# Differential attention: value products one more head behind the scores, a ring of eight half heads

## The chip, the cores and the metric

The kernel runs on one core of a Trainium2 chip, as one launch. The metric is the device time in microseconds of that launch, the median of several runs.

## The reference

The program is two layers of a hybrid network over 8 sequences (B) of 512 tokens (T) with 256 channels (C): differential attention, routed local attention with experts, a state-space layer, experts again, a fully connected layer with quantised weights and a last attention. The change touches the first part alone, which computes, for 8 heads of two half heads each (16 channels per half head) with H = 8 and hd = 16:

```
q, k = apply_rotary(rmsnorm(x @ Wq.T)), apply_rotary(rmsnorm(x @ Wk.T))   # per half head
v = (x @ Wv.T).reshape(B, T, H, 2 * hd)
scores = where(causal, q @ k.T / sqrt(hd), -inf)
attn = softmax(scores)                       # (B, 2H, T, T)
attn = attn[:, :, 0] - lam * attn[:, :, 1]   # two half heads of one head
out = layernorm(attn @ v) * (1 - LAMBDA_INIT)
x = x + out.reshape(B, T, C) @ Wproj.T       # x is a layer norm of the residual on the way in
```

The softmax has no maximum in the kernel: it takes exponentials of the scores, and a column of ones beside v gives the sums.

## The kernel before

`diff_attention` is one block in which each engine runs its own program in order, with semaphores between them. All loops go over **slots**: slot s stands for half head s, 16 slots for a batch element (called a batch below), 128 for all. A job of batch b stands at slot 16 b plus an offset from a table; the offsets reach from -39 to 32, so three batches are in work at a time. In the text a cycle slot is a slot modulo 16.

TensorE (PE), per slot s, in this order:

- scores of head s // 2 + 1, in three units of two half heads each (L270): units 0 and 1 in even slots, unit 2 in odd ones. Two pairs of PSUM banks alternate, so a unit waits for the exponentials of the unit two before it.
- in even slots, between the units, the value products of one head (L285, 16 matmuls): before the change those of head (s - 2) // 2. They wait for the triangle masks of both half heads and for the copy of the head before it out of the one PSUM bank that they use.
- the odd jobs of the slot. They use three "odd" PSUM banks in turn, in the order of the sorted job list, so each job waits until the bank of the job three places ahead of it is emptied. The jobs: x (transpose the normalised rows, L299), qk and v (products of three float32r terms, L138), turn (transpose q and k, L316), back (transpose a head's value sums to tokens, L321), heads (transpose the attention result, L326), out (product with Wproj, L332).

ScalarE (ACT), per slot: first it empties the odd banks filled in the slot before (x L378, qk L385, v L390, the high part of a turn L397, heads L400), then it copies the value sums of a head (`heads_out`, L365), then come the roots (logarithm and exponential for rms, row and head norms, L406 to L421), then the exponentials of the slot's score units into the ring `pt` (L358). A ring entry is waited for until the value products that read it are done. The high part of turn n waits for the spill DMAs of turn n - 2, since `hi` and `lo` have two buffers.

GpSimd (POOL), per slot: its jobs (cast of x L584, squares of q and k into one buffer L590, rotary swaps L599, the stack DMAs L610 that bring spilled q and k back), and then the masks of one half head, `triangle(s + 1)`, L576 and L578.

VectorE (DVE), per slot: it empties the odd banks of the slot before (low part of a turn L453, back L460 to L468, out into the residual L472 and, after the second, the row statistics), then its jobs: statistics and normalisation of rows (L112), low part of x (L491), sums of squares (L498), the scaling of q and k (L506), rope (L511, L515), and the norm of the heads: mean (L522, L524), centre (L528), square (L532), var (L536) and scale (L540, L542).

SyncE issues the six spill DMAs of each turn (L248), and clears regions of memory for a later stage.

Around the change, the end of a batch's preparation is a run over three engines: in cycle slot 11 ScalarE computes the rms root (L411, L416); VectorE scales q and k in slots 12 and 13; GpSimd swaps in slots 13, 13, 14 and 15, and issues stack DMAs in slot 15 ahead of the fourth swap; VectorE does rope in slots 14 and 15 and normalises the next batch's rows in 15; in slot 16 it adds the first output product to the residual. The sorted odd jobs from cycle slot 13 on are, before the change: heads 0, heads 1, back (13); out 0, back (15); out 1, v 0 (16); back, v 1 (17); turn 0, x 0, x 1 (18); back, turn 1 (19); turn 2 (20); back, turn 3, qk 0 (21). After it: heads 0, heads 1, back (13); out 0, back (15); out 1 (16); back (17); v 0, turn 0, x 0, x 1 (18); back, v 1, turn 1 (19); turn 2 (20); back, turn 3, qk 0 (21).

Of the kernel before, what the change touches and what calls it, by code (L numbers as in the profile page):

```python
# [27 lines left out]
B, T, C = 8, 512, 256  # L28
# [98 lines left out]
DA_H = 8  # L127
# [15 lines left out]
def diff_attention(core, w, a, spill, beside, s_x, load_rows, load_tables):  # L143
# [5 lines left out]
    nc, ps = core.nc, core.ps  # L149
    NH = 2 * DA_H  # L150
    NS = B * NH
    RING, CHUNKS = 6, 4
    S_BANK, AV_BANK, ODD_BANK, NODD = 0, 4, 5, 3
    place_of = (0, 640, 1024, 512)
    unit_tiles = ((0,), (3, 1), (2,))
    units = ((0, T), (T, 2 * T), (2 * T, 2 * T + 2 * P))
    table = [(-30, "x", 0), (-30, "x", 1), (-27, "qk", 0), (-26, "qk", 1), (-25, "qk", 2), (-24, "qk", 3),
             (-16, "v", 0), (-15, "v", 1), (-14, "turn", 0), (-13, "turn", 1), (-12, "turn", 2), (-11, "turn", 3),
             (29, "heads", 0), (29, "heads", 1), (31, "out", 0), (32, "out", 1)]
    table += [(2 * hv + 5, "back", hv) for hv in range(DA_H)]  # L160
    vector_table = [(-39, "stats", 0), (-33, "normal", 0), (-28, "xlo", 0), (-25, "sum", 0), (-24, "sum", 1), (-23, "sum", 2), (-22, "sum", 3),
                    (-20, "rms", 0), (-20, "scaled", 0), (-20, "scaled", 1), (-19, "scaled", 2), (-19, "scaled", 3),
                    (-18, "rope", 0), (-18, "rope", 1), (-17, "rope", 2), (-17, "rope", 3),
                    (20, "mean", 0), (21, "centre", 0), (22, "square", 0), (23, "var", 0), (27, "scale", 0)]
    scalar_table = [(-37, "row", 0), (-21, "rms", 0), (27, "std", 0)]
    pool_table = [(-29, "xhi", 0), (-26, "square", 0), (-25, "square", 1), (-24, "square", 2), (-23, "square", 3),
                  (-19, "swap", 0), (-19, "swap", 1), (-18, "swap", 2), (-17, "swap", 3),
# [18 lines left out]
    with own, ctx:  # L186
        def sb(name, shape, dt=F32):
            return ctx.enter_context(nc.sbuf_tensor("da_" + name, shape, dt))
# [21 lines left out]
        mean, var = sb("mean", [P, NT * DA_H]), sb("var", [P, NT * DA_H])  # L210
# [19 lines left out]
        def filled(eng, job):  # L230
            eng.wait_ge(s_odd, place[job] + 1)

        with nc.Block() as block:
# [22 lines left out]
            def _(pe):  # L256
                def scores(hv, u):
                    b, h = divmod(2 * hv, NH)
                    g, p = h // 8, h // 2 % 4
                    if h % 8 == 0 and u == 0:  # L260
                        for i in (2 * g, 2 * g + 1):
                            pe.wait_ge(s_stack[i], 32 * (b + 1))
                    unit = 3 * hv + u
                    if unit >= 2:
                        pe.wait_ge(s_e, 2 * (unit - 1))
                    for j in unit_tiles[u]:
                        c0 = place_of[j] % T
                        for sub in range(2):
                            r = 64 * sub
                            last = nc.tensor.matmul(ps[:, S_BANK + 2 * (unit % 2) + sub, c0:c0 + T - j * P],  # L270
                                                    kT[g][r:r + DA_ROWS, p, j * P:(j + 1) * P],
                                                    qT[g][r:r + DA_ROWS, p, j * P:T], start=True, stop=True)
                    last.then_inc(s_s, 1)

                def values(hv):
                    b, h = divmod(hv, DA_H)
                    pe.wait_ge(s_tri, 2 * (2 * hv + 2))
                    if h == 0:
                        pe.wait_ge(s_v, 2 * b + 2)
                    if hv >= 1:  # L280
                        pe.wait_ge(s_osb, hv)
                    for j in range(NT):
                        for sub in range(2):
                            c0 = place_of[j]
                            last = nc.tensor.matmul(ps[64 * sub:64 * sub + 64, AV_BANK, j * P:T],  # L285
                                                    vx[b % 2][:, j, h, :], pt[:, (2 * hv + sub) % RING, c0:c0 + T - j * P],
                                                    start=(j == 0), stop=(j == NT - 1))
                    last.then_inc(s_av, 1)
# [48 lines left out]
                for s in range(first_slot, last_slot):  # L337
                    ahead = 0 <= s + 2 - s % 2 < NS
                    if ahead:
                        scores(s // 2 + 1, 2 * (s % 2))  # L340
                    if s >= 2 and s % 2 == 0 and (s - 2) // 2 < B * DA_H:
                        values((s - 2) // 2)
                    if ahead and s % 2 == 0:
                        scores(s // 2 + 1, 1)
                    for job in odd.get(s, ()):
                        fill(job)

            @block.scalar
            def _(act):
# [11 lines left out]
                def heads_out(hv):  # L361
                    act.wait_ge(s_av, hv + 1)
                    if hv >= 2:
                        filled(act, ("back", (hv - 2) // DA_H, (hv - 2) % DA_H))
                    nc.scalar.copy(osb[:, hv % 2, :], ps[:, AV_BANK, :]).then_inc(s_osb, 1)  # L365
# [37 lines left out]
                def root(kind, b):  # L403
                    if kind == "row":
                        act.wait_ge(s_mv, b + 1)
                        nc.scalar.activation(core.std[:, b, :], core.mv[:, b, :, 1], ACT.Ln, bias=core.eps[:, :], scale=1.0)  # L406
                        act.drain()
                        nc.scalar.activation(core.rstd[:, b, :], core.std[:, b, :], ACT.Exp, scale=-0.5).then_inc(s_std, 1)
                    elif kind == "rms":
                        act.wait_ge(s_sum, NT * (b + 1))  # L410
                        nc.scalar.activation(ssum[:, :, :], ssum[:, :, :], ACT.Ln, bias=core.rms_eps[:, :],  # L411
                                             scale=1.0 / DA_D)
                        act.drain()
                        if b:
                            act.wait_ge(s_qn, NT * b)
                        nc.scalar.activation(srcp[:, :, :], ssum[:, :, :], ACT.Exp, scale=-0.5).then_inc(s_rms, 1)  # L416
                    else:
                        act.wait_ge(s_var, b + 1)
                        nc.scalar.activation(var[:, :], var[:, :], ACT.Ln, bias=core.eps[:, :], scale=1.0 / 32)
                        act.drain()  # L420
                        nc.scalar.activation(var[:, :], var[:, :], ACT.Exp, scale=-0.5).then_inc(s_std2, 1)  # L421
# [8 lines left out]
                for s in range(first_slot, last_slot):  # L430
                    for job in odd.get(s - 1, ()):
                        empty(job)
                    if s >= 3 and (s - 3) % 2 == 0 and (s - 3) // 2 < B * DA_H:
                        heads_out((s - 3) // 2)
                    for kind, b, i in scalar_jobs.get(s, ()):
                        if kind != "row" or b:
                            root(kind, b)
                    if 0 <= s + 2 - s % 2 < NS:
                        for u in ((0, 1), (2,))[s % 2]:
                            exponentials(s // 2 + 1, u)  # L440
# [3019 lines left out]
```

## Time and profile before

| | us |
|---|---|
| median of 3 runs (4077.23 to 4085.93) | 4081.86 |
| the profiled execution | 4082.73 |
| its span | 4080.9 |
| TensorE matmul busy in the span | 3623.4 (89%) |
| VectorE busy | 2915.8 (71%) |
| ScalarE busy | 1929.7 (47%) |
| GpSimd busy | 1633.9 (40%) |
| mean granted TensorE clock, of full speed | 0.949 |

Busy shares are over all stages. The first stage is the first seventh of the span. Matmuls are pipelined, so busy TensorE time overlaps itself.

### The profile page before, as it was taken

To read this page: it belongs to the slowest core of one execution; us is meant where nothing else is said; L and a number is where in the kernel's file an instruction comes from. 1 tells how busy PE (TensorE), PEld (TensorE's weight loads), DVE (VectorE), ACT (ScalarE), POOL (GpSimd) and SP (SyncE) were. 2 spreads that over 40 slices of the span, in tenths; PEclk is the share of its full clock that TensorE was granted. 3 is DMA by queue.
4 is the path that set the end of the run, shared out by engine and by line. 5 is a ranking of instruction groups with operands and counts; after the bars stand their busy time and mean duration, and the time that the engine had idled before them with its cause. 6 is when DMAs were issued, how large, how long until landed. Compare 5 with 4: busy or idle time off the path is not lost. (4 is left out here: it accounts for less than half of the span.)

```text
span 4080.9 us, 60197 instructions
## 1 busy us (share of the span) xinstructions
PE 3623.4 (89%) x19256; PEld 2605.9 (64%) x19256; DVE 2915.8 (71%) x5355; ACT 1929.7 (47%) x4079; POOL 1633.9 (40%) x1485
## 2 busy tenths in 40 slices
PE   4888878999599999998799788987999899999998
PEld 3455557889488888887789634544666455554666
DVE  5777657676566666645677578886888676766998
ACT  3565644444455555544344344442444466656332
POOL 3776726454566666633555411101003445441000
PEclk8999979999899999998899889989999899999999
DMA  5999902565100000001266400002102444441000
GB/s 136 303 256 275 304 32 73 167 202 170 48 19 17 19 19 19 19 2 38 95 186 195 154 24 17 19 11 43 21 0 49 91 111 101 103 110 25 11 15 16
DMA packets 228874, 358.33 MB, mean 88 GB/s; under 512 B 36482, under 2 KB 132851, under 8 KB 221811
## 3 DMA queue, kind: packets, MB, share of 16 engines
q1 hardware_dynamic: 204038, 265.38, 22.4%
q0 software_dynamic: 24544, 89.36, 9.0%
q8 instruction: 147, 2.41, 0.3%
q14 instruction: 145, 1.18, 0.1%
HBM read 173.82 MB, written 172.20 MB: 85 GB/s over the span
## 5 line engine op out<-in xcount | busy, mean ns | idle before, releaser
L2895 DVE TENSOR_REDUCE ab_nmx<-banks 128x1 f32<-128x512 f32 x512 | 329.3, 684 | 136.6 <-PE banks L2682 134.2
L2826 ACT ACTIVATE ab_pt<-banks 128x512 f32<-128x512 f32 x512 | 283.2, 600 | 162.0 <-PE banks L2692 152.9
L1737 POOL TENSOR_TENSOR lb_pq<-lb_pq,lb_rr 128x512 f32<-128x512 f32 x192 | 206.2, 1077 | 305.1 <-DVE lb_rr L1598 301.7
L1463 ACT ACTIVATE lb_pq<-banks,lb_nmx 128x256 f32<-128x256 f32 x384 | 178.5, 470 | 230.0 <-DVE lb_nmx L1593 226.8
L2692 PE MATMUL banks<-ab_qT,ab_kT 128*128 128x512 f32 x512 | 253.2, 500 | 5.3 <-ACT ab_pt L2826 5.3
L358 ACT ACTIVATE da_pt<-banks 128x512 f32<-128x512 f32 (+1 forms) x384 | 179.1, 537 | 123.4 <-PE banks L270 119.1
L1593 DVE TENSOR_REDUCE lb_nmx<-banks 128x2 f32<-128x512 f32 x192 | 131.1, 683 | 146.5 <-PE banks L1315 145.2
L2682 PE MATMUL banks<-ab_kT,ab_qT 128*128 128x512 f32 x512 | 209.1, 411 | 18.5 <-DVE ab_nmx L2895 13.7
L285 PE MATMUL banks<-da_pt,da_vx 128*64 128x512 f32 (+3 forms) x1024 | 166.3, 470 | 34.4 <-POOL da_pt L578 30.8
L576 POOL TENSOR_TENSOR da_pt<-da_pt,w_da_tri 128x384 f32<-128x384 f32 x128 | 150.4, 1175 | 87.0 <-ACT da_pt L358 86.9
L2466 PE MATMUL banks<-w_f_dT,f_hT 128*128 128x256 f32 x768 | 178.3, 382 | 4.0 <-ACT f_hT L2512 4.0
L2692 PEld LDWEIGHTS banks<-ab_qT,ab_kT 128*128 128x128 f32 x512 | 98.0, 193 | 131.1 <-ACT ab_pt L2826 77.2
L928 ACT ACTIVATE moe_b_h_raw<-banks,moe_b_b 128x512 f32<-128x512 f32 x124 | 85.0, 688 | 196.2 <-PE banks L138 165.5
L928 ACT ACTIVATE moe_a_h_raw<-banks,moe_a_b 128x512 f32<-128x512 f32 x124 | 84.7, 688 | 196.5 <-PE banks L138 163.3
L2441 PE MATMUL banks<-w_f_gT,f_xT 128*128 128x512 f32 (+1 forms) x512 | 169.6, 474 | 6.1 <-DVE f_both L2555 3.1
L2466 PEld LDWEIGHTS banks<-w_f_dT,f_hT 128*128 128x128 f32 x768 | 146.8, 192 | 38.1 <-ACT f_hT L2512 5.2
L2441 PE MATMUL banks<-w_f_uT,f_xT 128*128 128x320 f32 (+1 forms) x512 | 161.9, 459 | 0.0
L285 PEld LDWEIGHTS banks<-da_pt,da_vx 128*64 128x64 f32 x1024 | 76.5, 145 | 126.5 <-issue 77.5
L2490 ACT ACTIVATE f_sg<-banks 128x704 f32<-128x704 f32 x64 | 48.5, 758 | 205.2 <-PE banks L2441 205.2
L138 PE MATMUL banks<-moe_a_w_hi,moe_a_h_hi 128*128 128x256 f32 x496 | 144.0, 290 | 0.0
L138 PE MATMUL banks<-moe_b_w_hi,moe_b_h_hi 128*128 128x256 f32 x496 | 144.0, 290 | 0.0
L138 PE MATMUL banks<-moe_b_w_lo,moe_b_h_hi 128*128 128x256 f32 x496 | 141.3, 285 | 0.0
(538 smaller groups left out, 11180.4 us busy)
## 6 DMA issues: line engine op xcount, KB each, us to landing
moe_xs<-zero SPq DMA_DIRECT2D x71, 512.0 KB, 11.5
moe_ys<-zero SPq DMA_DIRECT2D x71, 512.0 KB, 11.5
moe_a_w_raw<-in_moe_w SPq DMA_DIRECT2D x48, 512.0 KB, 3.9
moe_b_w_raw<-in_moe_w SPq DMA_DIRECT2D x48, 512.0 KB, 3.8
da_spill<-da_hi SPq DMA_DIRECT2D x128, 128.0 KB, 2.4
ab_spill<-ab_hi SPq DMA_DIRECT2D x128, 128.0 KB, 2.4
ab_qT<-ab_spill POOLq DMA_DIRECT2D x32, 392.0 KB, 5.8
ab_kT<-ab_spill POOLq DMA_DIRECT2D x32, 392.0 KB, 5.5
```

Of the source, the lines that this page charges most:

```text
L138: done = core.nc.tensor.matmul(bank, a[i], b[j], start=(first and n == 0), stop=(last and n == len(terms) - 1))
L285: last = nc.tensor.matmul(ps[64 * sub:64 * sub + 64, AV_BANK, j * P:T], vx[b % 2][:, j, h, :], pt[:, (2 * hv + sub) % RING, c0:c0 + T - j ...
L358: nc.scalar.activation(pt[:, n % RING, c0:c1], ps[:, S_BANK + 2 * (unit % 2) + sub, 0:c1 - c0], ACT.Exp, scale=1.0 / math.sqrt(DA_D)).then ...
L928: nc.scalar.activation(h_raw[:, m % 2, :], ps[:, UP_BANK + n % 3, :], ACT.Gelu, bias=b1[:, load_of[i] % 2, m:m + 1]).then_inc(s_g, 1)
L1463: nc.scalar.activation(pq[:, n % RING, t, :], ps[:, S_BANK + n % 2, 2 * P * t:2 * P * t + 2 * P], ACT.Exp, bias=nmx[:, n % RING, t:t + 1], ...
L1737: nc.gpsimd.tensor_tensor(pq[:, n % RING, :, :], pq[:, n % RING, :, :], bcast(rr[:, n % RING, :], 2, 2 * P), ALU.mult).then_inc(s_p, 1)
L2441: last = nc.tensor.matmul(ps[:, bank, at:at + size], self.xT[:, k, c, :], w[key][:, c, c0:c0 + size], start=(c == 0), stop=(c == KC - 1))
L2466: last = nc.tensor.matmul(ps[:, 3, 0:C], self.hT[:, k, m, :], w["f4_dT"][:, m, :], start=False, stop=(m == F4_IC - 1))
L2682: nc.tensor.matmul(ps[:, MAX_BANK + n % 3, :], half.q[:, par, p, qt * P:(qt + 1) * P], half.k[:, p, :], start=True, stop=True).then_inc(s_ ...
L2692: nc.tensor.matmul(ps[:, EXP_BANK + n % 3, :], half.k[:, p, j * P:(j + 1) * P], half.q[:, par, p, :], start=True, stop=True).then_inc(s_s, 1)
L2826: nc.scalar.activation(pt[:, s % RING, :], ps[:, EXP_BANK + s % 3, :], ACT.Exp, scale=AB_D ** -0.5).then_inc(s_e, 1)
L2895: nc.vector.tensor_reduce(nmx[:, g % 2, col:col + 1], ps[:, MAX_BANK + n % 3, :], op=ALU.max, axis=AX.X, negate=True).then_inc(s_mx, 1)
```

## The change

The ring of exponentials has eight entries instead of six. The value products of a head, its copy by ScalarE and its transposes back come two slots (one head) later relative to the scores. The two v products of a batch, and mean, centre, square and var of the head norm, also stand two slots later; scale and the jobs behind it stay.

```diff
-    RING, CHUNKS = 6, 4
+    RING, CHUNKS = 8, 4
...
-             (-16, "v", 0), (-15, "v", 1), (-14, "turn", 0), (-13, "turn", 1), (-12, "turn", 2), (-11, "turn", 3),
+             (-14, "v", 0), (-13, "v", 1), (-14, "turn", 0), (-13, "turn", 1), (-12, "turn", 2), (-11, "turn", 3),
...
-    table += [(2 * hv + 5, "back", hv) for hv in range(DA_H)]
+    table += [(2 * hv + 7, "back", hv) for hv in range(DA_H)]
...
-                    (20, "mean", 0), (21, "centre", 0), (22, "square", 0), (23, "var", 0), (27, "scale", 0)]
+                    (22, "mean", 0), (23, "centre", 0), (24, "square", 0), (25, "var", 0), (27, "scale", 0)]
...
-                    if s >= 2 and s % 2 == 0 and (s - 2) // 2 < B * DA_H:
-                        values((s - 2) // 2)
+                    if s >= 4 and s % 2 == 0 and (s - 4) // 2 < B * DA_H:
+                        values((s - 4) // 2)
...
-                    if s >= 3 and (s - 3) % 2 == 0 and (s - 3) // 2 < B * DA_H:
-                        heads_out((s - 3) // 2)
+                    if s >= 5 and (s - 5) % 2 == 0 and (s - 5) // 2 < B * DA_H:
+                        heads_out((s - 5) // 2)
```

## Rows read from the trace of the kernel before

**Rows 1.** The page: span and number of instructions.
```profile
span 4080.9 us, 60197 instructions
```
**Rows 2.** Waits of TensorE, 85 to 500 us: total us, times, longest.
```profile
PE banks L285 <- POOL da_pt L578: 30.6, 14, 4.9
PE banks L138 <- DVE residual L472: 7.9, 5, 2.5
PE banks L138 <- DVEq L455: 6.8, 6, 2.4
```
**Rows 3.** Timeline of TensorE, 303 to 331: start, duration, idle before.
```profile
304.54 2.37 PE L285 MATMUL banks<-da_pt,da_vx 128*64 128x512 f32 x16 [0.30 <-POOL da_pt L578]
...
314.31 3.69 PE L285 MATMUL banks<-da_pt,da_vx 128*64 128x512 f32 x16 [4.01 <-POOL da_pt L578]
...
322.95 0.39 PE L138 MATMUL banks<-da_wv_hi,da_xT_hi 128*128 128x256 f32 x1 [2.54 <-DVE residual L472]
323.18 0.28 PE L138 MATMUL banks<-da_wv_lo,da_xT_hi 128*128 128x256 f32 x1
323.30 0.28 PE L138 MATMUL banks<-da_wv_hi,da_xT_lo 128*128 128x256 f32 x1
```
**Rows 4.** Timeline of GpSimd, 299 to 324.
```profile
304.44 3.41 POOL L599 TENSOR_TENSOR da_rot<-da_qk,w_da_sin 128x512 f32<-128x512 f32 x2
...
310.41 1.59 POOL L599 TENSOR_TENSOR da_rot<-da_qk,w_da_sin 128x512 f32<-128x512 f32 x1 [0.68 <-issue]
...
314.20 1.05 POOL L610 DMA_DIRECT2D da_qT<-da_spill  x2
...
316.27 1.28 POOL L599 TENSOR_TENSOR da_rot<-da_qk,w_da_sin 128x512 f32<-128x512 f32 x1
```
**Rows 5.** Timeline of VectorE, 299 to 324.
```profile
317.58 1.89 DVE L511 TENSOR_TENSOR da_qk<-da_qk,w_da_cos 128x512 f32<-128x512 f32 x1 [2.78 <-POOL da_rot L599]
...
322.22 0.68 DVE L472 TENSOR_TENSOR residual<-banks,residual 128x512 f32<-128x512 f32 x1
```
**Rows 6.** TensorE in a stretch: bounds, length, busy, granted clock, DMA share, GB/s.
```profile
193.00:197.00 4.00, 4.00 (x16) 0.50 1.05 408
```
**Rows 7.** Timeline of TensorE, 126 to 152.
```profile
133.02 3.89 PE L285 MATMUL banks<-da_pt,da_vx 128*64 128x512 f32 x16 [4.18 <-POOL da_pt L578]
...
141.78 0.39 PE L138 MATMUL banks<-da_wv_hi,da_xT_hi 128*128 128x256 f32 x1 [1.88 <-DVE da_t L463]
...
148.16 0.66 PE L316 MATMUL banks<-ident,da_qk 128*128 128x128 f32 x4
```
**Rows 8.** Timeline of TensorE, 430 to 446.
```profile
438.65 4.54 PE L285 MATMUL banks<-da_pt,da_vx 128*64 128x512 f32 x16 [4.92 <-POOL da_pt L578]
```
**Rows 9.** VectorE by line, 85 to 500: count, busy us, mean ns, idle before.
```profile
L528 DVE TENSOR_TENSOR da_att<-da_att,da_mean 128x1024 f32<-128x1024 f32 x6 | 9.9, 1647 | 0.8
```
**Rows 10.** Timeline of VectorE, 282 to 300.
```profile
291.77 1.09 DVE L498 TENSOR_REDUCE da_ssum<-da_sq 128x32 f32<-128x512 f32 x1 [1.27 <-POOL da_sq L590]
...
296.93 1.07 DVE L498 TENSOR_REDUCE da_ssum<-da_sq 128x32 f32<-128x512 f32 x1
```
**Rows 11.** Timeline of ScalarE, 294 to 302.
```profile
299.16 0.39 ACT L411 ACTIVATE da_ssum<-da_ssum,rms_eps 128x128 f32<-128x128 f32 x1
```
**Rows 12.** Timeline of TensorE, 456 to 468.
```profile
462.22 2.37 PE L285 MATMUL banks<-da_pt,da_vx 128*64 128x512 f32 x16 [1.62 <-ACT da_osb L365]
```
**Rows 13.** Timeline of TensorE, 71 to 95.
```profile
85.59 3.71 PE L285 MATMUL banks<-da_pt,da_vx 128*64 128x512 f32 x16 [3.00 <-POOL da_pt L578]
...
90.20 1.04 PE L299 MATMUL banks<-ident,x_normed 128*128 128x128 f32 x8
```
**Rows 14.** Timeline of VectorE, 85 to 92.
```profile
86.01 3.28 DVE L112 TENSOR_SCALAR x_normed<-residual,mean_var,rstd 128x256 f32<-128x256 f32 x4
```
**Rows 15.** Timeline of VectorE, 527 to 546.
```profile
536.08 0.20 DVE L460 RECIPROCAL da_rr<-banks 128x8 f32<-128x8 f32 x1
...
537.36 1.22 DVE L522 TENSOR_REDUCE da_mean<-da_att 128x32 f32<-128x1024 f32 x1
```

## The prediction, made before the changed kernel ran

> **What bounds the kernel now.** I read the page's span first, then the waits of TensorE inside the first stage, then the timelines of TensorE, GpSimd, VectorE and ScalarE over one batch. The change touches only the first stage, differential attention, in a span of 4080.9 us [rows 1]. TensorE works nearly without a break there, and its largest idle group is the value products waiting for the triangle masks of GpSimd: 30.6 us in 14 waits; behind it stand 7.9 us for VectorE's residual add and 6.8 us for a bank that VectorE empties [rows 2]. So the change aims at the largest wait. The question is whether that wait is the cause or only the first place at which TensorE meets something late.
>
> In one batch [rows 3]: the value products of cycle slot 14 start at 304.54, those of slot 16 at 314.31 after 4.01 us of idling, and TensorE idles again, 2.54 us, before the v product at 322.95. GpSimd in the meantime is not idle. It works through the rotary swaps with the masks queued between them: two swaps from 304.44 for 3.41 us, a third at 310.41, then the issue of four stack DMAs from 314.20 to 316.27, and the fourth swap, done at 317.55 [rows 4]. VectorE waits 2.78 us for that swap, runs rope and the normalisation of the next rows, and only then, at 322.22, adds the output product to the residual, which frees an odd bank at 322.90 [rows 5]. I call this run, from the roots on ScalarE in slot 11 to the residual add in slot 16, the ladder. Both waits of TensorE are waits for the same ladder, the first part way along, the second at its end.
>
> **The change part by part.**
>
> *Value products two slots later, ring of eight.* Value products of slot 16 now need the masks made two pool slots earlier (before the swaps that start at 304.44), so the 4.0 us wait goes, in each of the six ladders. The count of products, exponentials and masks stays. The two added ring entries keep the wait of the exponentials for a free entry at the same slot distance.
>
> What is late next: the odd banks rotate by three in the order of the job list. Before, the v product (slot 0) stood three behind output product 0, and so waited for the residual add. After, that place belongs to the transposes back of slot 1. TensorE was ready for the slot 16 values at 314.31 - 4.01 = 310.30. They take 2.37 us at the full clock (as at 304.54). Scores and output product behind them took from 318.00 (314.31 + 3.69) to 320.41 (322.95 - 2.54), so 2.4 us; the score unit of slot 17 is 0.4. TensorE arrives at the bank at 315.5 and waits until 322.9, some 7.4 us [rows 3]. GpSimd and VectorE have the same instructions in the same order within the ladder, and none of them waits for TensorE there (VectorE's one wait is for GpSimd), so nothing ends it earlier. The gain per batch is only what TensorE does before the new wait and did behind the old one: one score unit, 0.4 us.
>
> *The clock.* After each of the six 4 us waits TensorE ran at its half level: a window of 4 us after one of them has a granted clock of 0.50 (1.2 of 2.4 GHz) [rows 6]. The value products there took 3.89 us in the first and 4.54 us in the last of six [rows 7, 8], 4.2 in the mean, instead of 2.37 [rows 3]: 1.8 us lost. So far this is hidden, because TensorE idles for the ladder's end 2.5 us afterwards. With one wait of 7 us at the end of the ladder the slow products come behind it, and from there to the next roots TensorE sets the pace. Cost +1.8 per batch, less 0.3 for the slow v products that one batch already had. Bounds: 0 to +2.7 (all of the next 6 us slow).
>
> The Trainium skill, "TensorE: Matmul & The Clock Gate", section "Why this matters for your kernels", warns of idle gaps of TensorE between bursts of matmuls, after which it runs at its lower clock. The rule speaks against a change that joins two gaps into one long one with work right behind it: by it the five regular ladders cost their 1.8 us each, while with a clock that does not mind the gap the sum below would be 9 us lower. The trace agrees with the rule (0.50 after the 4.0 us gap).
>
> *Statistics two slots later.* mean, centre, square, var move from cycle slots 4 to 7 to slots 6 to 9, among the four sums of squares and the row statistics. They add mean (1.22 [rows 15]) and centre (1.65 [rows 9]) plus a small multiply and drains, 3.2 us, ahead of the fourth sum. VectorE idled 1.27 us there for GpSimd's square, and the fourth sum ended at 298.00, 1.16 us before the root that reads it [rows 10, 11]. 3.2 - 1.27 - 1.16 = 0.8 us by which roots, and with them the ladder, start later. The square buffer is single, so GpSimd's squares shift too, but the masks queued behind them now have two slots to spare. Five ladders have this: +4.0 (bounds 0 and 3.6 each, if shared-port slowing stretches all four). ScalarE's wait for var has two slots left, enough in the loop.
>
> *v products two slots later.* v0 joins the turn and x jobs in slot 2, v1 those in slot 3; ScalarE's two copies move along. The x cast on GpSimd now waits for v1 of slot 3, about when the x copies end plus one product; the low part on VectorE is needed two slots later, so I cost this at nothing. If that cover is gone it is at most 1.5 us per batch. v1 now lies between turn 0 and turn 2, whose high part waits for the spill DMAs of turn 0. TensorE's waits for turn 2's bank, 6.8 us in six and up to 2.4 [rows 2], fall to a floor of some 0.65 (exponentials and subtraction): -2.9. In the last batch with turns, the value products waited 1.62 us behind ScalarE, which had waited for the same DMA [rows 12]: -1.3.
>
> *The first ladder* has no output products yet. There TensorE waited at 141.78 for a bank and started turn 0 at 148.16 [rows 7]; after the change turn 0 is what waits, and starts near 141.8, with v1 still to come (twelve matmuls 0.12 us apart, 1.4 us [rows 3]) and 1.8 slow: -3.2.
>
> *Start.* Before, TensorE waited 3.0 us before the first value products (85.59), and the x transposes began at 90.20 [rows 13]. After, only v0 and turn 0 stand in front of the x transposes, which need the rows that VectorE normalises until 89.29 [rows 14], a gain of 0.9; v1 then follows at 1.4 to 2.8 (half clock), and the first value products have moved out of this stretch to be paid at the end: +1.3, between 0.5 and 1.9.
>
> *End.* The last head's transposes back come one job later behind the final row statistics. One head's combining on VectorE takes 1.28 us (from 536.08 to the mean at 537.36) [rows 15]; less what moves elsewhere, +1.2.
>
> **The sum.** Five regular ladders: -0.4 + 1.8 - 0.3 = +1.1 each, +5.5; roots +4.0; first ladder -3.2; turn banks -2.9; last turns -1.3; start +1.3; end +1.2. Together +4.6 us. The profiled execution took 4082.73 us around its span of 4080.9; with the change 4087.3 and 4085.5. The three timed runs have their median at 4081.86, 0.9 below the profiled one, so I predict 4086.5.
>
> **The rivals.**
>
> *A: the wait of the value products simply goes.* Then -30.6 us and little behind: with the start and the end paid (+2.5): 4054. For it: it is the largest wait, and its release is a mask that gets two more slots. Against it: the second wait, for the residual add, shows that TensorE catches the ladder's end anyway. A milder form keeps the new wait but pays no slow clock (-9.0) and has no late roots (-4.0): 4073.5.
>
> The Trainium skill, "Perfetto Trace Analysis", section "Optimization Strategy", says that one and the same gap repeated on the engine that should be saturated can mean too few buffers. By it the larger ring is the cure, and the time is A's; the trace bears it out only for the ring, and not for the three odd banks, whose number stays.
>
> *B: VectorE becomes the bound in slots 6 to 10, slower than before.* The statistics sit between the chained squares and sums. If VectorE and GpSimd stretch each other (centre takes 1647 ns in the mean over these batches [rows 9]), the fourth sum comes up to 3.6 us late in five ladders, and each such delay passes into the ladder whole: +14 over my +4, and with the turn gain eaten, +17: 4103. It decides as soon as the fourth sum is more than about 2 us behind the arrival of ScalarE. Against it: idle time on VectorE there, and the lighter slots 4 and 5.
>
> *C: the forecast at its dear end.* The slow clock comes out at its upper bound (5 times 0.9 more) and the turn banks give nothing (2.9): 4086.5 + 7.4 = 4094.
>
> **How the numbers follow.** A run can be told from no change at about 0.2%, 8.2 us. My forecast has 0.46. A has 0.14, its milder form 0.10, B 0.18, C 0.12. The forecast's own range is 4078 to 4094. To hold 8 in 10 the range must reach well into A and B: 4062 to 4101. Faster by over 0.2% (below 4073.7): A and most of the milder form, 0.22. Slower (above 4090.0): B, most of C, the upper part of the forecast, 0.34. The rest, 0.44, is no change.
>
> **What would show it.** Right: no wait of the value products for the mask in slot 16; instead one of 6 to 8 us of the transposes back (ident, osb) for the residual add, once per batch from the second ladder on; value products of 3.5 to 4.5 us right behind it; from the roots to the residual add still 23 to 24 us. Late roots would show as a wait of ScalarE's da_ssum for VectorE. Wrong: if the new wait is under 4 us with the clock full, or the residual add comes sooner after the roots, A is right; if ScalarE waits over 2 us at the roots, B.

## The result and the profile after

| | before | after |
|---|---|---|
| median, us | 4081.53 (4073.7 to 4086.3, 6 runs) | 4100.9 (4094.93 to 4105.42, 6 runs) |
| after / before, with its 95% interval | | 1.005 (1.0035 to 1.0064) |
| the profiled execution, us | 4082.73 | 4101.23 |
| its span, us | 4080.9 | 4099.5 |
| last residual add of the first stage ends at, us | 554.5 | 574.5 |
| mean granted TensorE clock | 0.949 | 0.944 |

The change costs 19.4 us (14 to 26 by the interval). The forecast was 4.6 us dearer, 4086.5, with a range from 4062 to 4101; the measured time lies at its dear end. In the two traces the whole difference lies in the first stage: it ends 20.0 us later, and what follows takes 3526.4 us before and 3525.0 after. Here and below, "the first stage to" gives the end of its last residual add in the traced execution, which is one execution of each kernel.

The span, against [rows 1]:

```profile
span 4099.5 us, 60133 instructions
```

TensorE's waits from 85 to 520 us (total, times, longest), against [rows 2]:

```profile
PE banks L321 <- DVE residual L472: 52.8, 5, 10.7
...
PE banks L316 <- DVE da_t L463: 7.0, 1, 7.0
...
PE banks L138 <- DVEq L455: 2.5, 5, 0.5
...
PE banks L285 <- POOL da_pt L578: 0.4, 1, 0.4
```

The 30.6 us of waiting for the masks are gone to 0.4, and the waits for the turns' bank fell from 6.8 to 2.5. In their place stands what the prediction named, the transposes back waiting for the residual add, five times, once in each regular ladder. But it is 10.7 us long (10.0 in the last) and not 7.4. The single wait of 7.0 us is that of the first ladder, at turn 0.

TensorE in the same batch as [rows 3] (start, duration, idle before):

```profile
324.19 0.39 PE L270 MATMUL banks<-da_qT,da_kT 48*128 48x256 f32 x2
335.29 1.12 PE L321 MATMUL banks<-ident,da_osb 128*128 128x128 f32 x4 [10.71 <-DVE residual L472]
...
337.06 3.91 PE L285 MATMUL banks<-da_pt,da_vx 128*64 128x512 f32 x16
```

The clock behind that wait, against [rows 6] (bounds, length, busy, granted clock, DMA share, GB/s):

```profile
336.00:340.00 4.00, 4.00 (x12) 1.29 (x13) 3.60 (x15) 1.09 (x2) 0.00 (x0) 0.50 1.07 266
```

The granted clock is 0.50 (1.2 of 2.4 GHz), and the value products take 3.91 us here; in the five regular ladders 3.30, 3.71, 3.91, 4.02 and 4.53, 3.9 in the mean.

Where the 3.3 us between 7.4 and 10.7 come from is read off GpSimd and VectorE. First the root on ScalarE that starts the ladder, 9.6 us later than in [rows 11]:

```profile
308.77 0.39 ACT L411 ACTIVATE da_ssum<-da_ssum,rms_eps 128x128 f32<-128x128 f32 x1
```

VectorE from the fourth rope on, against [rows 5]:

```profile
327.22 4.58 DVE L511 TENSOR_TENSOR da_qk<-da_qk,w_da_cos 128x512 f32<-128x512 f32 x1 [2.77 <-POOL da_rot L599]
331.88 1.32 DVE L515 TENSOR_TENSOR da_qk<-da_qk,da_rot 128x512 f32<-128x512 f32 x1
333.13 1.51 DVE L112 TENSOR_SCALAR x_normed<-residual,mean_var,rstd 128x256 f32<-128x256 f32 x4
334.56 0.68 DVE L472 TENSOR_TENSOR residual<-banks,residual 128x512 f32<-128x512 f32 x1
```

GpSimd beside it, from the fourth swap on, against [rows 4]:

```profile
325.92 1.27 POOL L599 TENSOR_TENSOR da_rot<-da_qk,w_da_sin 128x512 f32<-128x512 f32 x1
327.14 1.00 POOL L576 TENSOR_TENSOR da_pt<-da_pt,w_da_tri 128x384 f32<-128x384 f32 x1
328.09 0.45 POOL L578 TENSOR_TENSOR da_pt<-da_pt,w_da_tri 128x128 f32<-128x128 f32 x1
328.50 0.98 POOL L576 TENSOR_TENSOR da_pt<-da_pt,w_da_tri 128x384 f32<-128x384 f32 x1
329.45 0.44 POOL L578 TENSOR_TENSOR da_pt<-da_pt,w_da_tri 128x128 f32<-128x128 f32 x1
...
331.22 1.43 POOL L576 TENSOR_TENSOR da_pt<-da_pt,w_da_tri 128x384 f32<-128x384 f32 x1
```

Behind its fourth swap the kernel before has two masks:

```profile
317.50 1.01 POOL L576 TENSOR_TENSOR da_pt<-da_pt,w_da_tri 128x384 f32<-128x384 f32 x1
...
318.86 1.45 POOL L576 TENSOR_TENSOR da_pt<-da_pt,w_da_tri 128x384 f32<-128x384 f32 x1
```

Now four masks, of a large and a small product each, follow the fourth swap without a pause. VectorE's rope product, which started 0.08 us behind the first of them, took 4.58 us; in [rows 5] the same instruction took 1.89. The first three masks run at their own speed (1.0 and 0.45 us), the fourth is slow (1.43): VectorE's product ended at 331.80, 0.58 us into it, and it takes 0.69 us where nothing is beside it (run 1), so it got through only about there. Before, two masks stood there, since the exponentials of the next ones weren't made: ScalarE got their scores from TensorE after the late value products. After, TensorE had run ahead, and ScalarE's last exponentials of these slots started before the swap. ScalarE before, then after:

```profile
318.53 1.08 ACT L358 ACTIVATE da_pt<-banks 128x512 f32<-128x512 f32 x2 [7.11 <-PE banks L270]
```

```profile
324.62 0.66 ACT L358 ACTIVATE da_pt<-banks 128x256 f32<-128x256 f32 x2 [0.68 <-PE banks L270]
```

From root to residual add the ladder took 23.1 us before (299.16 to 322.22) and takes 25.8 after (308.77 to 334.56). The line of this product over all six ladders (115 to 480 us; count, busy us, mean ns, idle before), before and after:

```profile
L511 DVE TENSOR_TENSOR da_qk<-da_qk,w_da_cos 128x512 f32<-128x512 f32 x24 | 32.8, 1368 | 17.8 <-POOL da_rot L599 17.8
L511 DVE TENSOR_TENSOR da_qk<-da_qk,w_da_cos 128x512 f32<-128x512 f32 x24 | 49.1, 2047 | 17.8 <-POOL da_rot L599 17.8
```

The same 24 instructions take 16.3 us more, 2.7 in each of the six ladders.

### The profile page after: what moved, and what is told of

It is laid out like the page before. It is cut to its first block and busy times, and to the rows that moved or that the text cites. A ratio compares the mean times of both kernels' runs of the same rounds, so it can differ in the third digit from the quotient of the medians.

```text
span 4099.5 us, 60133 instructions
## 1 busy us (share of the span) xinstructions
PE 3620.8 (88%) x19193; PEld 2610.1 (64%) x19256; DVE 2924.6 (71%) x5355; ACT 1931.7 (47%) x4079; POOL 1631.3 (40%) x1485
## 5 line engine op out<-in xcount | busy, mean ns | idle before, releaser
L138 PE MATMUL banks<-moe_b_w_hi,moe_b_h_lo 128*128 128x256 f32 x496 | 141.4, 285 | 0.0
```

Of the source, the lines that this page charges most:

```text
L138: done = core.nc.tensor.matmul(bank, a[i], b[j], start=(first and n == 0), stop=(last and n == len(terms) - 1))
```

## The experiments

In the expectations, **M** is the theory above: the masks that TensorE's earlier scores set free run beside the fourth rope and lengthen the ladder by 2.7 us, and TensorE waits at the ladder's end. Its rivals put the loss elsewhere: **S** with the moved statistics, which would make the roots late, **V** with the moved v products, and **C** with the slow clock behind the long wait. Each run is compared with the kernel before as timed on the same chip (its median in brackets); the kernel after was not timed beside them, so against it the traced first stages are set side by side. The rows of TensorE's waits are of 85 to 500 us.

**1. hold_masks**: after, with the masks kept back until the fourth rope is done.

```diff
                     for kind, b, i in pool_jobs.get(s, ()):
                         jobs_of[kind](b, i)
+                        if kind == "swap" and i == 3:
+                            pool.wait_ge(s_rope, NT * (b + 1))
```

> The changed kernel, and GpSimd waits for the fourth rope before it goes on to the masks behind the fourth swap. Theory M (the changed kernel lost its time because four masks in a row now run beside the fourth rope and stretch it, which makes the run from the roots to the residual add 2.7 us longer, and TensorE waits for the end of that run): the two rope instructions fall from 6.0 to about 1.5 us, the residual add comes some 4.4 us sooner in each of six batches, and the time falls by about 26 us, to 4075, below the kernel before. Rivals S (the moved statistics), V (the moved v products) and C (the slow clock behind the long wait) put the loss elsewhere: 4101 within 4, since the same masks only come later.

Measured: 4077.47 (before 4080.46), ratio 0.9993 (0.9983 to 1.0002); first stage to 549.9. VectorE, and the mask on GpSimd that waited:

```profile
315.61 0.69 DVE L511 TENSOR_TENSOR da_qk<-da_qk,w_da_cos 128x512 f32<-128x512 f32 x1 [2.77 <-POOL da_rot L599]
316.37 0.69 DVE L515 TENSOR_TENSOR da_qk<-da_qk,da_rot 128x512 f32<-128x512 f32 x1
316.98 2.87 DVE L112 TENSOR_SCALAR x_normed<-residual,mean_var,rstd 128x256 f32<-128x256 f32 x4
319.77 0.68 DVE L472 TENSOR_TENSOR residual<-banks,residual 128x512 f32<-128x512 f32 x1
```

```profile
317.14 1.10 POOL L576 TENSOR_TENSOR da_pt<-da_pt,w_da_tri 128x384 f32<-128x384 f32 x1 [1.57 <-DVE da_qk L515]
```

TensorE's largest wait:

```profile
PE banks L321 <- DVE residual L472: 35.6, 5, 7.5
```

The ladder is back at 22.6 us (root at 297.2), the wait at the 7.5 us that the prediction had (7.4), and the first stage 24.6 us shorter than after's. One added wait on GpSimd takes back all that the change cost. The rope product alone takes 0.69 us; the collision has moved to the normalisation (2.87 instead of 1.51), which is cheaper. C falls with this run too: the value products behind the wait are as slow as before (3.87 us here, 3.91 in after), and the time is gone all the same.

**2. v_only**: before, with the v products two slots later alone.

```diff
-             (-16, "v", 0), (-15, "v", 1), (-14, "turn", 0), (-13, "turn", 1), (-12, "turn", 2), (-11, "turn", 3),
+             (-14, "v", 0), (-13, "v", 1), (-14, "turn", 0), (-13, "turn", 1), (-12, "turn", 2), (-11, "turn", 3),
```

> The kernel before with the two v products two slots later, nothing else of the change. M: the mask wait of 4.0 us stays; the residual add's wait moves from the v product to the transposes back and stays near 2.1 us; start +3.6 (v between turn 0 and turn 1), turn banks -3 to -4: 4078 to 4085. V: most of the +19 comes with this part: 4095 or more.

Measured: 4079.44 (4080.46), ratio 0.9993 (0.9977 to 1.001). TensorE keeps its mask wait and meets the residual add at the transposes back:

```profile
PE banks L285 <- POOL da_pt L578: 32.1, 13, 6.4
PE banks L321 <- DVE residual L472: 13.0, 4, 3.8
```

So the order of the odd jobs alone, which moves the residual wait to L321, costs nothing that the medians show, and V falls as the cause of 19 us. The traced execution (4087.28) is one of the longest of the ten, with the first stage to 560.3, 5.7 later than before, and it holds a small form of M. The rope product is as before (1.89), but two more masks follow a little later and stretch the normalisation:

```profile
326.70 3.07 DVE L112 TENSOR_SCALAR x_normed<-residual,mean_var,rstd 128x256 f32<-128x256 f32 x4
```

```profile
327.17 0.99 POOL L576 TENSOR_TENSOR da_pt<-da_pt,w_da_tri 128x384 f32<-128x384 f32 x1
```

The regular ladders but the last are 24.0 to 24.7 us long, not 23.1, and the wait is 2.8 to 3.8 us where about 2.1 had been expected.

**3. stats_only**: before, with mean, centre, square and var two slots later alone.

```diff
-                    (20, "mean", 0), (21, "centre", 0), (22, "square", 0), (23, "var", 0), (27, "scale", 0)]
+                    (22, "mean", 0), (23, "centre", 0), (24, "square", 0), (25, "var", 0), (27, "scale", 0)]
```

> The kernel before with mean, centre, square and var two slots later, nothing else. M: 0 to +4 us (roots at most 0.8 us later in five batches): 4081 to 4086. S: VectorE is late at the roots by 2 to 3 us per batch and the time is 4093 to 4100, with ScalarE's da_ssum waiting for VectorE.

Measured: 4083.3 (4080.46), ratio 1.0007 (0.9997 to 1.0018); first stage to 558.2, 3.7 later than before; no wait of ScalarE at the roots. The interval (-1 to +7 us) is far from 19 us, and S falls. The 3.7 us are no measure of late roots either: 3.4 of them are there at the root at 121.92 (118.57 before), and the first of the moved statistics runs at 163.27, so up to there the two kernels do the same. What the move does to the roots is seen behind the last q and k product: the root starts 6.4 us after its end before, and 6.7 to 6.8 here (7.7 in the last batch).

**4. late_empty**: after, with the fourth rope and the normalisation one slot later, behind the emptying of the bank.

```diff
-    vector_table = [(-39, "stats", 0), (-33, "normal", 0), (-28, "xlo", 0), (-25, "sum", 0), (-24, "sum", 1), (-23, "sum", 2), (-22, "sum", 3),
+    vector_table = [(-39, "stats", 0), (-32, "normal", 0), (-28, "xlo", 0), (-25, "sum", 0), (-24, "sum", 1), (-23, "sum", 2), (-22, "sum", 3),
...
-                    (-18, "rope", 0), (-18, "rope", 1), (-17, "rope", 2), (-17, "rope", 3),
+                    (-18, "rope", 0), (-18, "rope", 1), (-17, "rope", 2), (-16, "rope", 3),
```

> The changed kernel with the fourth rope and the normalisation one slot later, so that VectorE empties the first output product and the transposes back in front of them, in the 2.8 us in which it idles for the fourth swap. M: TensorE no longer waits at the transposes back of slot 1 but at turn 0 of slot 2, with about 5.3 us more of its work done before the wait, in five batches: -26 us, 4075. If the odd bank is not what holds TensorE, the time stays at 4101; if the slow clock C is the whole cost, it stays within 5 us of 4101 too, since a wait over 4 us remains.

Measured: 4078.84 (4080.46), ratio 0.9992 (0.9981 to 1.0004); first stage to 551.9. TensorE's waits:

```profile
PE banks L316 <- DVE residual L472: 24.1, 5, 5.1
...
PE banks L299 <- DVE da_t L463: 8.2, 5, 2.0
...
PE banks L321 <- DVE residual L472: 3.4, 5, 1.2
```

The residual add is no longer behind the fourth rope, and the value products that follow L321 are back at 2.37 us. But TensorE now waits for the next bank, and VectorE's line shows why: its small product that combines two half heads has met the fourth swap and the four masks instead.

```profile
316.74 5.65 DVE L468 SCALAR_TENSOR_TENSOR da_att<-da_t,da_nlam 128x128 f32<-128x128 f32 x1
```

The mean of this line (115 to 480 us) is 634 ns before and 1003 ns here. GpSimd ran the swap from 316.83 and the masks from 318.07, and VectorE's product ended at 322.39, just behind the start of the fourth mask (322.20). What counts is the row of masks, not which product of VectorE stands there.

**5. after_all_three**: after with the edits of runs 1 and 4, and the stack DMAs 2 and 3 one slot later, so that the fourth swap doesn't stand behind 2.05 us of issuing.

```diff
-                  (-1, "stack", 2), (-1, "stack", 3)]
+                  (0, "stack", 2), (0, "stack", 3)]
```

> The changed kernel with three edits: masks held until the fourth rope is done, the fourth rope and the normalisation one slot later, and the last two stack loads of a batch one slot later, behind the fourth swap. Theory M: the ladder ends some 5.5 us sooner than with the late rope alone (3.3 from the masks, 2.1 from the loads), TensorE waits at most 1 to 2 us per batch, and the time falls to 4045 to 4055. If TensorE's own work or ScalarE were the bound by then, it stays at 4065 to 4075.

Measured: 4060.07 (4077.64), ratio 0.9953 (0.9937 to 0.9969); first stage to 538.3, 57.7 us for a batch in place of 64.5.

```profile
PE banks L299 <- DVE da_t L463: 14.7, 5, 3.4
PE banks L138 <- DVEq L455: 10.3, 5, 8.3
```

With run 11 it is the fastest kernel of the study, faster than both. The expectation was 5 to 15 us lower; part of what is missing is in these two waits. The first, 3.4 us in each regular batch, is for a bank that VectorE empties behind the residual add and its row statistics. Of the second, 8.3 us are a single wait in the first ladder, which has no residual add: VectorE's low part waits there for ScalarE's high part, and that for a spill DMA (waits between 134 and 158 us):

```profile
ACT da_hi L397 <- DMA da_spill<-da_hi: 7.7, 1, 7.7
```

Why this DMA is late isn't shown; run 7, with the stack edit alone, has such a wait of 4.1 us at the same place.

**6. before_all_three**: the same three edits, to the letter, on the kernel before.

> The same three edits on the kernel before. M: the wait of the value products for their mask stays at 3 to 4 us per batch, since that mask stands ahead of the fourth swap and its wait; only the wait for the residual add (7.9 us in all) goes: 4069 to 4075. So the change under study is worth some 20 us once the ladder is short. Rival (the change is of no use in any setting): this kernel and the one with the change take the same time within 4 us.

Measured: 4071.23 (4077.64), ratio 0.9989 (0.9979 to 0.9998).

```profile
PE banks L285 <- POOL da_pt L578: 33.2, 15, 5.0
```

As expected in itself: the mask wait stays, so the shorter ladder gives little. The difference to run 5, what the change is worth once the ladder is short, is 11 us in the medians; in the traced first stages it is only 2.7 (541.0 and 538.3). Some 20 had been expected. This run's profiled execution, 4062.75, is the shortest of its nine, so the medians are the better measure; their intervals against the kernel before don't overlap.

**7. after_stacks_late**: after with the stack edit of run 5 alone.

> The changed kernel with only the last two stack loads one slot later. M: the fourth swap comes 2.07 us sooner, and as nothing but the ladder bounds a batch, so does everything behind it, in six batches: 4088 to 4090. If the ladder does not bound: 4101.

Measured: 4074.72 (4077.64), ratio 0.999 (0.9981 to 1.0); first stage to 551.2. VectorE, then GpSimd:

```profile
315.23 1.46 DVE L511 TENSOR_TENSOR da_qk<-da_qk,w_da_cos 128x512 f32<-128x512 f32 x1 [1.16 <-POOL da_rot L599]
316.77 0.79 DVE L515 TENSOR_TENSOR da_qk<-da_qk,da_rot 128x512 f32<-128x512 f32 x1
317.48 3.17 DVE L112 TENSOR_SCALAR x_normed<-residual,mean_var,rstd 128x256 f32<-128x256 f32 x4
```

```profile
316.11 0.90 POOL L578 TENSOR_TENSOR da_pt<-da_pt,w_da_tri 128x128 f32<-128x128 f32 x1
316.95 1.05 POOL L610 DMA_DIRECT2D da_qT<-da_spill  x2
```

The expectation counted the 2.05 us that the swap comes sooner, in each of six batches, 11 to 13 us; the first stage is 23.3 us shorter than after's, about twice that. The issue of the DMAs now stands between the first mask and the other three, so only one mask meets the rope product (1.46 us). The edit does two things at once and by itself takes back the loss; for M it is a second witness, by another way than the wait of run 1.

**8. after_v_start**: after with the v products of batch 0 at their old slots.

```diff
-                slots.setdefault(NH * b + at, []).append((kind, b, i))
+                at_b = at - 2 if kind == "v" and b == 0 else at
+                slots.setdefault(NH * b + at_b, []).append((kind, b, i))
```

> The changed kernel with the v products of the first batch alone at their old slots. At the start, v1 between turn 0 and turn 1 makes the second turn's spill later, and the first roots of the loop came 3.9 us later than before instead of 1.3. M with this part: -2.4 us, 4098.5, and the second turn copy 2.4 us sooner after the first. If the start is late for another reason (the larger ring, loads), nothing changes.

Measured: 4092.27 (4077.64), ratio 1.0036 (1.0022 to 1.005), which overlaps with the 1.005 (1.0035 to 1.0064) of after; first stage to 572.4, 2.1 less than after. ScalarE's high parts of the first four turns (durations, first to last start), in the kernel before, in after, and in this run, whose lines are one further on:

```profile
L397 ACT CAST da_hi<-banks x4: 585/586/586, 47.2 to 58.0; 128x512 fp32r<-128x512 f32 x4
```

```profile
L397 ACT CAST da_hi<-banks x4: 586/586/586, 48.4 to 61.6; 128x512 fp32r<-128x512 f32 x4
```

```profile
L398 ACT CAST da_hi<-banks x4: 585/585/585, 46.8 to 57.6; 128x512 fp32r<-128x512 f32 x4
```

From the first turn to the fourth it is 10.7 us before, 13.2 in after and 10.7 here: with v1 between turns 0 and 1 the turns of the first batch end 2.5 us later, and here that is gone. This is shown; what it is worth in the whole time is not. The five timed runs don't tell 4092 from 4098, and the 2.1 us of the first stage, near the expected 2.4, are within what two executions differ by (3.4 us at the third root between before and run 3, with the same instructions up to there).

**9. before_hold**: before with the wait of run 1.

```diff
+                        if kind == "swap" and i == 3:
+                            pool.wait_ge(s_rope, NT * (b + 1))
```

> The kernel before, with masks held until the fourth rope is done and nothing of the change. M: the two rope instructions fall from 3.3 to about 1.5 us, the residual add comes 1.8 us sooner, and of the 2.5 us wait behind it most goes: -1.8 in each of five batches, less a little clock, so the first stage ends 6 to 9 us sooner: 4070 to 4074 beside 4079. A rival by which the masks cost nothing beside the rope: no change.

Measured: 4077.33 (4078.32), ratio 0.9995 (0.9986 to 1.0004).

```profile
PE banks L285 <- POOL da_pt L578: 32.6, 14, 4.9
```

A miss: 6 to 9 us had been expected and 1 was found, within the noise. The rope product falls to 0.69 us, but the masks now stand beside the normalisation:

```profile
325.00 2.88 DVE L112 TENSOR_SCALAR x_normed<-residual,mean_var,rstd 128x256 f32<-128x256 f32 x4
```

So the ladder is 22.6 us long where it was 23.1: 0.5 us shorter, not 1.8. The residual wait is 5.1 instead of 7.9 us. One batch of this trace (182.4 to 245.2, root to root) is 62.8 us long and the next 60.0: in the long one TensorE waits 2.1 us and not 0.8 for the bank of turn 2, and runs the q and k products behind that wait at the low clock (0.57 from 223.2 to 227.2 us). Before the change there was little to win by holding the masks back, since two masks stood there and not four.

**10. after_hold_stacks**: after with the edits of runs 1 and 7.

> The changed kernel with masks held and the last two stack loads one slot later, the fourth rope at its own slot. M: both edits shorten the same ladder, and their gains add up to about 6 us per batch until TensorE's wait at the transposes back (10.7 us) is near 4: first stage 10 us shorter than with the held masks alone: 4066. If something else bounds by now (TensorE's own work), as near 4075 as with one of them.

Measured: 4069.04 (4078.32), ratio 0.9978 (0.9969 to 0.9987).

```profile
PE banks L321 <- DVE residual L472: 24.8, 5, 5.3
```

The first stage ends at 541.9, 8.0 us before that of run 1, where 10 had been expected. The wait shrinks from 7.5 to 5.3 us, near the 2.05 us of issuing that left the ladder. The wait at the ladder's end is the ladder's length less the time TensorE has work for.

**11 and 12. after_three_late_stats** and **before_three_late_stats**: runs 5 and 6 with the row statistics after the second output product in a later slot (34), behind the emptying of a transposed-back head.

```diff
-                        if i == 1:
-                            dve.drain()
-                            token_stats(core, dve, b)
+                def out_stats(b, i):
+                    dve.drain()
+                    token_stats(core, dve, b)
```

> The changed kernel with the three edits, and the row statistics after the second output product moved behind the next transposes back. With the three edits TensorE waits 3.4 us per batch for the bank of those transposes, which VectorE empties only after 3.4 us of statistics. M (it is always the odd bank behind VectorE's queue): that wait falls to 0.5 or less, -3 us in five batches: first stage 12 to 15 us shorter, 4046. Rival (from here on TensorE's own work bounds): within 4 us of 4060.

> The same four edits on the kernel before. Its waits are for masks (33 us), and no bank waits behind the statistics: no change, 4068 to 4073. With the run beside it this prices the change under study once nothing waits for banks: M expects 20 to 25 us in its favour, the rival under 8.

Measured: 4062.42 (4078.32), ratio 0.9951 (0.9938 to 0.9965), and 4075.77, ratio 0.9987 (0.9977 to 0.9997); first stages to 536.7 and 558.5. TensorE in run 11:

```profile
PE banks L321 <- DVEq L455: 13.7, 4, 3.4
```

A miss for run 11: no gain over run 5. The wait of 14.7 us at L299 is gone and 13.7 us stand at L321, for the low part of a turn, which VectorE does right behind the moved statistics (their last copy starts at 318.82, the low part at 319.39). Moving the statistics past one bank put them in front of the next. The two runs differ by 13 us in the medians: the second estimate, after the 11 of runs 5 and 6, of what the change gives with a short ladder. In the traced first stages it is 21.8, but run 12's traced execution (4084.99) is the longest of its eleven. M had expected 20 to 25, the rival view that the change is worth nothing under 8: it is in between.

## Why the prediction was wrong

**The step that failed** is the sentence "GpSimd and VectorE have the same instructions in the same order within the ladder, and none of them waits for TensorE there (VectorE's one wait is for GpSimd), so nothing ends it earlier": it took the ladder's length as fixed, and put a longer ladder at nothing. Its first half is true of the ladder's own instructions. But the masks queued behind the fourth swap are not of the ladder, they wait for ScalarE's exponentials and through them for TensorE; with TensorE unblocked they came four in a row. I had said 23 to 24 us, and measured are 25.8 (24.7 in the last): 2.7 us in each of six, 16.3 in all, against a miss of 15.4 in the stage (20.0 less 4.6). Shown by run 1, which adds one wait and gets the ladder back to 22.6 us and the stage to 549.9, and by run 7 in another way. Rival B said 4103, and the measured 4100.9 is near it by luck: it had another cause.

The row that should have warned stood in [rows 5]: the rope product took 1.89 us where the residual add of the same size took 0.68, and the trace has GpSimd's two masks (317.50 to 321.18) beside the long one. I bounded no term from it.

The Trainium skill, "SBUF — State Buffer", section "SBUF: two separate sides", has the rule: a VectorE instruction with two SBUF inputs and a GpSimd one that reads SBUF exclude each other, and whichever starts second waits for the whole of the other's instruction. The trace agrees in kind (0.69 us alone, 4.58 beside masks), but goes further than one instruction: VectorE stood back through six of GpSimd's.

**The wait that takes the place of the old one**: right in its place, its count (five) and its kind, and wrong in size by the same step. 7.4 + 2.7 from the ladder, and 0.5 because TensorE came to the bank 15.8 us behind the root (324.58 against 308.77) instead of 16.3, make 10.6 of the measured 10.7; with the ladder short it was 7.5.

**The clock**: right. 0.50 behind the wait, and value products of 3.9 us in the mean where 2.37 + 1.8 = 4.2 was said. Run 4, where the long gap stands elsewhere, has them at 2.37. No run isolates what the clock costs, but two batches of the trace before do, by chance. In both TensorE does the same work behind the root (299.16 and 362.73) and comes out of its wait for the residual add 23.8 us behind it. Then, 0.8 us later, the clock falls in the first and not in the second (TensorE: bounds, length, busy, granted clock, DMA share, GB/s):

```profile
323.70:327.70 4.00, 4.00 (x21) 0.57 1.24 219
387.20:391.20 4.00, 4.00 (x31) 1.00 1.18 222
```

The next value products start 1.5 us later, and behind them TensorE waits 2.42 us and not 0.73 for the bank of turn 2: the batch takes 63.6 us, the other 60.4. It is the batch from which [rows 3] was read, the longest of the regular ones. The kernel after has no such difference: its regular batches take 64.0 to 64.8 us.

**Start**: +1.3 said, +3.9 measured between the two traces (the second root at 70.0 and 73.6, the third at 118.6 and 122.5). I counted one product behind the transposes of x; but v1 stands between turns 0 and 1, and in the first batch nothing covers it, and the fourth turn comes 2.5 us later (run 8). How much of the 3.9 is the change's is open: 1.2 us are there at the very first root (33.24 and 34.40), and run 3 is 3.4 us behind before at the third root with the same instructions up to there.

**Roots**: +4.0 said, and in the kernel after they are not late at all: the fourth sum ends at 307.63, the root starts at 308.77, as far apart as in [rows 10, 11], and it starts 6.4 us behind the end of the last q and k product in both kernels. With that rival B's mechanism is false: no wait of ScalarE at the roots. With the statistics moved alone (run 3) they are 0.3 to 0.4 us late, and 1.3 in the last batch.

**Turn banks**: 6.8 to 2.5 us of waiting, -4.3 where -2.9 was said. **Last turns**: the wait of 1.62 us is gone (at most 0.2 now), -1.4 where -1.3 was said. **First ladder**: -3.8 against -3.2, before its own +2.7 (from the root at 118.57 or 122.47 to the next it is 57.8 us and not 58.9). **End**: +1.0 against +1.2 (from the end of the last row statistics to the mean it is 3.6 us and not 2.5). Without ladder, start, first ladder and end, the traced roots leave +2.8 for what the terms from the score unit to the last turns put at +5.3; the roots' +4.0 came to nothing, so the others of these were together 1.5 us too low.

The terms as measured: start 3.9, ladders 16.3, first ladder -3.8, the regular batches' rest 2.8, end 1.0: 20.2, and the first stage is 20.0 longer. The rest is what the others leave, so that the sum closes proves nothing; the 16.3 is measured by itself.

**Rival A** and its milder form are false: TensorE does catch the ladder's end, with a longer wait than before.

**Still open**: what lets VectorE in. In three traced cases VectorE's product ended 0.2 to 0.6 us into the last mask of a row (which starts at 331.22 in after, 322.20 in run 4, 318.86 in before); whether a pause between GpSimd's instructions or an empty queue decides was not tried. No run has the value products moved alone, so how many of the four masks that part sets free by itself isn't shown. Open too is what the change is worth with a short ladder: 11 and 13 us in the medians, 2.7 and 21.8 in the traces. The regular batches of run 6 take 58.0 to 58.9 us in its trace, those of run 12 58.5 to 62.1; in run 12's two longest TensorE waits 2.6 and 2.1 us for the bank of turn 2 and its clock is at the low level behind that. With the change (runs 5 and 11) this wait is 0.5 us in every regular batch.

## What to carry to other kernels

A wait removed from an engine that meets the same run of work twice moves to that run's end: shorten the run first (runs 5, 6, 10), then give the buffers. And ask what the engine that you unblock sets free: work of a helper engine that used to come later may fall on top of the critical run. Where GpSimd and VectorE both read operands in SBUF, place GpSimd's free work with a wait on the critical product, or spread it, rather than let it come when it is ready.

## What the runs showed of the hardware

- A VectorE product of two SBUF operands, 128x512, takes 0.69 us alone, 1.46 to 1.89 beside one or two of GpSimd's masks, 4.58 beside four in a row. A 128x128 one took 5.65 us beside a swap and four masks, where its mean before was 0.63 (five times, run 4).
- GpSimd pays little: the two products of a mask take 1.0 and 0.45 us alone, 1.43 and 0.9 when VectorE gets in. Beside rows of masks it is VectorE that loses: 3.9 us on one instruction, against 0.45 of GpSimd's.
- The normalisation, one SBUF operand, is stretched as well: its four instructions take 1.51 us with a mask beside the first 0.4 us, 2.2 to 3.2 beside masks for longer (runs 1, 2, 5, 7, 9).
- Two levels of TensorE's clock show in one kernel's neighbouring batches: 16 value products take 2.37 us at a granted clock of 1.00, and 3.30 to 4.54 behind gaps of 4.0 to 10.7 us, where all or part of them run at 0.50. The same v products are 0.12 us apart in one batch and 0.21 in another, in stretches with 1.00 and 0.57.
